# Places for 2304 instead of 2560 edges in a sender block: the fifth tile of each block spread over 128 partitions as two pairs of slots

## The reference, cut to what matters

```python
h = relu(x @ proj.T + b)                                # block 0, two message passes
for l in range(2):
    trans = einsum('nh,tdh->tnd', h, edge_W[l])
    agg = segment_sum(trans[edge_type, src], dst)
    h = relu(gru_cell(agg, h, ...))
x = layernorm(x + h @ out_w.T + out_b)
# block 1, three passes: messages W_r x[src], mean for each (type, target), root, residual
for W, root, b in ...:
    agg = segment_sum(xw[etype, src] * norm[:, None], dst)
    h = res + relu(relu(agg + h @ root + b))
x = layernorm(x + h)
x = layernorm(x + gcn(x))                               # block 2, sums at the senders, scaled by degrees
x = layernorm(x + mlp([x, mean attributes at sender, mean attributes at target]))   # block 3
```

## Time and profile before

| | |
|---|---|
| median of 3 runs | 2967.55 us (2962.49 to 2968.0) |
| the profiled execution, span from first to last instruction | 2969.2 us |
| PE busy | 2492.2 us (84%) |
| DVE busy | 1808.3 us (61%) |
| POOL busy | 1585.9 us (53%) |
| ACT busy | 868.5 us (29%) |
| chain that ended last | PE 69%, issue 10%, DMA 7%, DVE 6% |
| transfers | 520.11 MB, mean 175 GB/s |

### The profile page before, as it was taken

How to read it: one execution, slowest core, us unless ns; L and a number is a source line. 1 busy time by engine, 2 the same in 40 slices (tenths; PEclk the granted TensorE clock), 3 DMA queues, 4 the chain that set the end, 5 groups by cost and what they waited for, 6 DMA issues and landing times.

```text
span 2969.2 us, 45704 instructions
## 1 busy us (share of the span) xinstructions
PE 2492.2 (84%) x15625; PEld 2211.7 (74%) x15625; DVE 1808.3 (61%) x6126; ACT 868.5 (29%) x1546; POOL 1585.9 (53%) x1706
## 2 busy tenths in 40 slices
PE   7587878888687899746999998998989897878798
PEld 3366666666387889436999997888988886777797
DVE  4565656575576777423876655676865554433585
ACT  2355555554354111213222231111311110443102
POOL 0656666663577666542566626666456665565200
PEclk9789888888799999857999999999999999898899
DMA  7312112110398666106888887877788774565793
GB/s 273 111 50 53 51 51 53 51 52 25 103 281 260 166 173 170 38 27 210 274 272 270 269 266 231 240 228 211 238 273 251 226 234 134 174 213 198 232 267 105
DMA packets 271515, 520.11 MB, mean 175 GB/s; under 512 B 61999, under 2 KB 115554, under 8 KB 270501
## 3 DMA queue, kind: packets, MB, share of 16 engines
q1 hardware_dynamic: 185053, 289.49, 31.2%
q0 software_dynamic: 86224, 227.59, 26.6%
HBM read 323.93 MB, written 192.99 MB: 174 GB/s over the span
## 4 chain that ended last, share of the span: by engine, by line
PE 69%; issue 10%; DMA 7%; DVE 6%; another core or an unknown queue 4%; ACT 2%; POOL 2%; SPq 0%; DVEq 0%; POOLq 0%; ACTq 0%
PE ps L1058 21%; PE ps L1030 10%; PE ps L892 7%; PE ps L1043 6%; PE ps L1245 5%; PE ps L1289 4%; PE ps L886 4%; PE ps L878 4%; DMA chunks<-xs 2%; DMA rec<-chunks,idx 2%; DMA srow<-lanes_of_slots 1%; DVE shot L2033 1%; POOL attributes L744 1%; PE ps L1112 1%
## 5 line engine op out<-in xcount | busy, mean ns | idle before, releaser
L735 POOL DMA_INDIRECT rec<-chunks,idx x596 | 588.5, 987 | 500.5 <-PE ps L1058 184.9
L1058 PE MATMUL ps<-dhot,rec 128*128 128x168 f32 x4768 | 757.2, 312 | 70.4 <-issue 35.3
L1058 PEld LDWEIGHTS ps<-dhot,rec 128*128 128x128 f32 x4768 | 703.8, 194 | 99.6 <-issue 77.6
L2054 DVE TENSOR_SCALAR dhot<-iota,dcode 128x168 f32<-128x168 f32 x2384 | 584.6, 311 | 216.7 <-remote 102.4
L1030 PE MATMUL ps<-hrow,shot 126*128 126x128 f32 x4000 | 516.3, 284 | 63.8 <-issue 29.5
L735 POOL DMA_INDIRECT msg<-messages,idx_buf x416 | 398.2, 957 | 307.3 <-issue 189.7
L1030 PEld LDWEIGHTS ps<-hrow,shot 126*128 126x128 f32 x4000 | 493.7, 199 | 81.7 <-issue 65.9
L1386 ACT ACTIVATE xs<-ps 128x512 f32<-128x512 f32 x500 | 295.1, 597 | 763.5 <-PE ps L1030 393.8
L744 POOL DMA_INDIRECT attributes<-w,rank_to x352 | 353.2, 1004 | 213.1 <-issue 102.2
L2033 DVE TENSOR_SCALAR shot<-srow,lane_no 126x512 f32<-126x512 uint8 x500 | 230.2, 486 | 117.4 <-PE ps L1030 51.2
L892 PE MATMUL ps<-big,lane1h 128*128 128x300 f32 x832 | 231.6, 432 | 9.3 <-issue 8.0
(11 more groups left out here) (304 smaller groups left out, 2538.6 us busy)
## 6 DMA issues: line engine op xcount, KB each, us to landing
chunks<-xs SPq DMA_DIRECT2D x375, 256.0 KB
tmp<-inverse_counts SPq DMA_DIRECT2D x36, 1008.0 KB
chunks<-xs SPq DMA_DIRECT2D x125, 258.0 KB
srow<-lanes_of_slots SPq DMA_DIRECT2D x100, 320.0 KB
grec<-chunks SPq DMA_DIRECT2D x125, 256.0 KB
messages<-big SPq DMA_DIRECT2D x25, 504.0 KB
trow<-lanes_of_targets SPq DMA_DIRECT2D x30, 320.0 KB
rec<-chunks,idx POOLq DMA_INDIRECT x596
```

The source lines that it names most:

```text
L735: eng.indirect_dma_start(buf, None, table, bass.IndirectOffsetOnAxis(ap=index, axis=0)).then_inc(sem, 16)
L1058: last = mm(ps[:, 4 + i % 2, (v % 3) * WT:(v % 3 + 1) * WT], rec[:, v % RS, j * P:(j + 1) * P], dhot[:, v % DS, j * WT:(j + 1) * WT], star ...
L2054: last = vec.tensor_scalar(dhot[:, v % DS, j * WT:(j + 1) * WT], iota[:, 0:WT], dcode[:, v, j:j + 1], None, ALU.is_equal)
```

## The change

A block now has 2304 places: four tiles of 128 records and a fifth of 64 records. The fifth tile's 64 records of 4 slots are laid over 128 partitions with 2 slots each: partitions 0 to 63 hold slots 0 and 1, partitions 64 to 127 slots 2 and 3. So the fifth tile has 2 columns, in `srow`, `shot`, the products, ACT's copy, the codes and the one-hot rows of the senders' sums. In DRAM a record stays a row of 4 slots, so each half is stored and loaded by a transfer of its own with 64 rows. The last 12 rounds of the first loop work out the partition and column of ranks from 2048 on by six more steps.

```diff
-NTILE = NQ * 4
+FULL = NQ - TB
+NTILE = 4 * FULL + 2 * TB
+LANE_ROWS = -(-NTILE // 4)
-CAP = QS * SPAN
+HALF = P // 2
+BLOCK_RECS = (QS - 1) * P + HALF
+CAP = 4 * BLOCK_RECS
-RECS = NQ * P
+RECS = TB * BLOCK_RECS
...
+        def slot_cols(n):
+            return 4 if n < FULL else 2
+        def puts(k, n):
+            return 1 if n < FULL else 4 if k == 1 else 2
...
                 def store_tile(k, i):
+                    if n < FULL:
+                        eng.dma_start(x1_d[at:at + P, 0:cols], xs[:, i % XS, 0:cols])
+                    else:
+                        for z in range(2):
+                            lanes, to = slice(z * HALF, (z + 1) * HALF), slice(2 * z * P, 2 * (z + 1) * P)
+                            eng.dma_start(x1_d[at:at + HALF, to], xs[lanes, i % XS, 0:2 * P])
+                            if k == 1:
+                                codes = slice(4 * P + 2 * z, 4 * P + 2 * z + 2)
+                                eng.dma_start(x1_d[at:at + HALF, codes], xs[lanes, i % XS, 4 * P:4 * P + 2])
...
-            eng.dma_start(srow_d.rearrange("(i c) p -> c i p", c=NQ), srow_u8[0:NQ])
+            eng.dma_start(srow_d.rearrange("(i c) p -> c i p", c=LANE_ROWS), srow_u8[0:LANE_ROWS])
...
             for i in range(NQ):
+                if by_record(i) < FULL:
+                    eng.dma_start(to[:, 0:4 * P], x1_d[at:at + P, 0:4 * P])
+                    eng.dma_start(to[:, 4 * P:], attr_d[4 * at:4 * (at + P), :].rearrange(...))
+                else:
+                    rows_ = x1_d[at:at + HALF, 0:4 * P].rearrange("l (m z c) -> z l m c", z=2, c=2 * A)
+                    for z in range(2):
+                        eng.dma_start(to[lanes, 0:2 * P].rearrange("p (m c) -> p m c", c=2 * A), rows_[z])
+                        eng.dma_start(to[lanes, 2 * P:2 * (P + A)], attrs[z])
...
-                for j in range(4):
+                for j in range(slot_cols(tile_no(k, i))):
                     last = mm(ps[...], shot[...], hrow[0:BS, sb_, :], start=True, stop=True)
...
-                    act(xs[:, i % XS, 0:4 * P], ps[:, STAGE1_BANKS[i % 3], :], ACT.Copy)
+                    cols = slot_cols(tile_no(k, i)) * P
+                    act(xs[:, i % XS, 0:cols], ps[:, STAGE1_BANKS[i % 3], 0:cols], ACT.Copy)
...
+                    last_round = g >= NEAR_STEPS[-1]
+                    if last_round:
+                        st.did(vec.tensor_scalar(rank_i[:, 4, :], rank_i[:, 0, :], 1, 1, ...))
+                        st.did(vec.tensor_scalar(rank_half[:, 0, :], ranks_g, float(4 * P * (QS - 1)), None, ALU.is_ge))
...
+                        st.did(vec.tensor_tensor(rank_half[:, 1, :], rank_half[:, 0, :], rank_i[:, 4, :], ALU.mult))
+                        st.did(vec.tensor_tensor(rank_half[:, 0, :], rank_half[:, 0, :], src_sb[...], ALU.mult))
+                        st.settle()
+                        st.did(vec.scalar_tensor_tensor(out=slot_lane[...], in0=rank_half[:, 1, :], ...))
+                        st.do(vec.tensor_tensor(rank_half[:, 0, :], rank_half[:, 0, :], rank_half[:, 1, :], ALU.add))
+                        st.do(vec.scalar_tensor_tensor(out=rank_hi[:], in0=rank_half[:, 0, :], scalar=-2.0, ...))
```

More of the change, by code:

```diff
@@ L251, in graph_kernel @@
             no_rows = one("no_rows", [P, RANKS // P])
-            rank_i = one("rank_i", [P, 4, G], I32)
+            rank_i = one("rank_i", [P, 5, G], I32)
+            rank_half = one("rank_half", [P, 2, G])
             slot_lane = one("slot_lane", [P, SUB, G])
@@ L417, in every_fifth, with first_col, by_record, first_record @@
             return buf[:, first:first + YW * (NYB - 2) + 1:YW]
-        def tile_slots(i):
-            return (i % QS) * QCOLS + i // QS * 4
+        def slot_cols(n):
+            return 4 if n < FULL else 2
+        def first_col(n):
+            return 4 * n if n < FULL else 4 * FULL + 2 * (n - FULL)
+        def by_record(i):
+            return i % QS * TB + i // QS
+        def first_record(n):
+            return n % TB * BLOCK_RECS + n // TB * P
+        def puts(k, n):
+            return 1 if n < FULL else 4 if k == 1 else 2
+        def all_puts(s, runs):
+            return sum(puts(k, n) for k in range(1, runs + 1) for n in range(s, NQ, XS))
+        def put_wait(eng, k, i):
+            s = i % XS
+            eng.wait_ge(q(f"x1_stored_{s}"), 16 * (all_puts(s, k - 1) + sum(puts(k, n) for n in range(s, i + 1, XS))))
         def targets_got(eng, c):
@@ L430, in record_got @@
             s = i % GR
-            eng.wait_ge(q(f"x1_stored_{s}"), 16 * (4 * len(range(s, NQ, XS)) + 2 * (i // GR + 1)))
+            loads = sum(1 if by_record(n) < FULL else 2 for n in range(s, i + 1, GR))
+            eng.wait_ge(q(f"x1_stored_{s}"), 16 * (all_puts(s, 4) + 2 * loads))
         def record_put(eng, v):
@@ L866, in first_loop @@
                 eng.sem_inc(q("count_mm"), SUB)
-                mm(ps[:, 7, 0:NTILE], wt("ones"), lanes_flat[:, GE:GE + NTILE], start=True, stop=False, skip_group_check=True)\
+                mm(ps[:, 7, 0:QS * QCOLS], wt("ones"), lanes_flat[:, GE:GE + QS * QCOLS], start=True, stop=False,
+                   skip_group_check=True)\
                     .then_inc(q("placed"), 1)
@@ L1154, in _ @@
                     for j in range(4):
-                        last = mm(ps[0:NQ, 7, j * P:(j + 1) * P], src1[:, j * NQ:(j + 1) * NQ], wt("ident"), start=True,
-                                  stop=True)
+                        last = mm(ps[0:LANE_ROWS, 7, j * P:(j + 1) * P], src1[:, j * LANE_ROWS:(j + 1) * LANE_ROWS], wt("ident"),
+                                  start=True, stop=True)
                     last.then_inc(q("lanes_mm"), 1)
@@ L1286, in _ @@
                 record_got(eng, i)
-                for j in range(4):
-                    got = grec[:, i % GR, :].rearrange("p (m s a) -> p s m a", s=4, a=A)[:, j]
+                cols = slot_cols(by_record(i))
+                for j in range(cols):
+                    got = grec[:, i % GR, 0:cols * (P + A)].rearrange("p (m s a) -> p s m a", s=cols, a=A)[:, j]
                     last = mm(ps[0:BS, 6 + b % 2, 0:P + A], ghot[:, i % GH, j, :], got, start=first_tile and j == 0,
-                              stop=last_tile and j == 3)
+                              stop=last_tile and j == cols - 1)
                 last.then_inc(q("gcn_sum"), 1)
@@ L1382, in keep_tile @@
                     if i >= XS:
-                        slot_wait(eng, "x1_stored", XS, k, NQ, i - XS)
+                        put_wait(eng, k, i - XS)
                     elif k >= 3:
-                        slot_wait(eng, "x1_stored", XS, k - 1, NQ, range(i, NQ, XS)[-1])
-                    act(xs[:, i % XS, 0:4 * P], ps[:, STAGE1_BANKS[i % 3], :], ACT.Copy).then_inc(q("x1_evac"), 1)
+                        put_wait(eng, k - 1, range(i, NQ, XS)[-1])
+                    cols = slot_cols(tile_no(k, i)) * P
+                    act(xs[:, i % XS, 0:cols], ps[:, STAGE1_BANKS[i % 3], 0:cols], ACT.Copy).then_inc(q("x1_evac"), 1)
                 def keep_sums(k, gi):
@@ L2036, in slot_hot @@
                         after(eng, "shot", k, i + 1)
[L2037 removed]
+                        st.did(vec.tensor_reduce(deg_part[0:BS, n:n + 1], shot[0:BS, i % SS, 0:cols], AX.X, ALU.add))
                     if k == 1 and i in beside:
@@ L2211, in slot_hots @@
                     eng.wait_ge(q("gcn_sum"), i - GH + 1)
-                for j in range(4):
-                    at = tile_slots(i) + j
+                for j in range(slot_cols(by_record(i))):
+                    at = first_col(by_record(i)) + j
                     last = vec.tensor_scalar(ghot[:, i % GH, j, :], iota[:, 0:BS], gcn_lo[:, at:at + 1], None, ALU.is_equal)
```

75 lines of the change are left out of this document (49 added, 26 removed).

## The result

The changed kernel takes 3038.56 us (median of 4 runs, 3029.7 to 3068.16), the kernel before 2967.78 beside it: a ratio of 1.0243, 95% interval 1.0188 to 1.0298. That is 71 us slower, where I forecast 7, and above the range.

The account below looks back on a forecast made before the run. PE was taken as the limit in layer 2, with POOL also near its limit in layers 3 and 4, and SP next, close behind PE. Terms +16 +15 -27 +3 = +7 us on 2967.55 gave 2974; range 2940 to 2996.

Parts of the forecast that it names:

- two terms of the sum: Fifth tiles of layer 1 and sums at the senders, both longer through SP's issues: +16 and +15 us.
- The half transfer, 0.42 us: On SP, a 64-row transfer was taken to cost 0.42 us, between 0.30 for 25 rows and 0.48 for 128.
- Sums at the senders, +15: SP would need 6.19 us a block instead of 5.52, making this stage 15 us longer; bounds 7 less, 29 more.
- My special price for 512 pieces: At the sums at the senders, SP's next transfer was taken to start 0.62 us behind each load of 512 pieces.
- Products of layers 2 to 4, -27: Halved fifth-tile products on PE would save 11.2 us in layer 2 and 8 each in layers 3 and 4.
- First loop, +3: Six more small DVE steps in each of the last 12 rounds would add 3 us, bounds 0 and 9.
- At nothing: The store of the lanes (113 partitions instead of 125) and the shorter clearing of attributes would change nothing.
- SP is cheap for halves: Rival: 64 rows cost SP 0.30 us in layer 1 and the sums; -27 us, 2940; chance 0.22.
- SP sets nothing: Rival: POOL and ACT pace layer 1, transfer engines the sums at 5.04 us a block; -36 us, 2931; chance 0.04.
- POOL holds layers 3 and 4: Rival: only layer 2 gives its 11 us of saved products; +23 us, 2990; chance 0.15.
- Small pieces cost more: Rival: on SP, 0.83 us behind each 512-piece load and 0.48 for a half; +27 us, 2994; chance 0.12.
- 200 s - 53: Layer 1 plus sums at the senders, in us, with s the start to start of a half transfer on SP.

Follow-up runs that it names:

- e1: Changed kernel with 24 of layer 1's full tiles stored in several pieces of various lanes and columns; 3058.74 us in its one execution.
- e5: Changed kernel with ACT instead of SP issuing layer 1's second-half rows and codes of fifth tiles and all attribute loads at the sums; ratio 1.0047.
- e4: Kernel before with two of the four products of each fifth tile left out in layers 2 to 4, nothing else changed; ratio 1.0006.
- e7: Kernel before without the attribute sends of layers 2 to 4, all products kept; ratio 0.9402.
- e6: Kernel before with fifth tiles' products halved and the attribute sends left out in layers 2 to 4; ratio 0.9321.

## Why the prediction was wrong

**The direction was right, by two terms of the sum; its size was not.** 74 us were lost where I said 31, and 27 of gain that I set against them never came.

**The half transfer, 0.42 us: wrong, and out of its bounds.** I took 0.30 for 25 rows and 0.48 for 128 as ends and went between. It is 0.64, above both. In layer 1 100 x (0.64 - 0.42) = 22 us are the whole distance from the 984.0 forecast for the first gather to 1006.38. The mechanism (SP's four issues a tile, ACT and POOL waiting for stores, the gather behind them) was as described; the term was mis-sized. The step that failed is the assumption that the cost rises with rows, so that neighbours in row count bound it; e1 shows 32 and 128 lanes at 0.42 and 64 at 0.59.

**Sums at the senders, +15: +33.** The four half loads take 2908.61 - 2905.96 = 2.65 us, not 2.08, and the transfer behind them 0.63 from start to start instead of 0.48. That is 0.72 more a block, 18 us over 25, the miss. My special price for 512 pieces (0.62, measured 0.65) happened to be near; it is no property of the pieces, since rows and attributes cost the same, and stores of 1 KB rows too. The floor by the transfer engines, 5.04 us a block, was not refuted: e5 ends at 132.7, 5.3 a block, with them 0.90 busy.

**Products of layers 2 to 4, -27: about 0.** e4 measured the term alone: 1.0006. I had read that PE is the limit in layer 2 from its 74.00 busy of 74.00 us, and that POOL is not from 48.70 busy of 74. Both rows are true, and the conclusion was not. PE was at its pace there: 567 records in 80 us before, 573 in 80 in e7, 495 in 70 in e6, 7.1 to 7.2 a us, but 496 in 79 in e4, 6.3. So a second chain, one that goes with the sends, was as long as PE's work, and I gave the whole of PE's saving. POOL's 48.70 busy of 74 do not show that chain. What PE alone would give was reckoned well for layer 2, 11.2 us against the 10 of e6; that 27 for three layers is near the 26.2 of e6 is luck, as the 8 us of layers 3 and 4 were set by POOL's floor. In layers 3 and 4 I saw POOL near its floor, and took 8 of at most 9 us all the same. The bound from below should have been 0, as the rival's reason applied to all layers.

**First loop, +3: nothing.** Its last L946 starts at 741.2, L892 at 741.7 before. DVE's 96.46 us instead of 88.59 put nothing off.

**At nothing:** right for lanes and attributes: the first tile's product starts at 805.0, 806.7 before.

**The rivals.** SP is cheap for halves: out, with 0.60 an issue and 0.64 from start to start. SP sets nothing: out, by e5, which gives 39.6 us of the sums back by moving issues alone. POOL holds layers 3 and 4: the gain did not come there, and not in layer 2 either; e7 shows that POOL's sends have a part in it. Small pieces cost more: right in sign. The true case is both of these and a dearer half transfer, and I had priced each rival with the other terms left at their middle. With 0.64 in my own formula, 200 s - 53, the two SP terms give 75 us, against 74 measured. Its mechanism holds; that it fits so closely is partly luck, since it gives 38 to layer 1 (40.6) and 37 to the sums (33.3), where it has 0.2 us behind 512 pieces that is not there. And with the products at about 0 the whole is 200 s - 50, which changes sign at s = 0.25 and not at 0.38: by it even the cheap half transfer of 0.30 would have made the kernel slower.

## What to carry to other kernels

Before a transfer is split into partition halves, count its issues on its queue: each costs the queue a fixed time, here more than that of the whole. Spread them over a second engine that is idle in that stage before the saving on the bound engine is booked. And where an engine is busy all the time, ask whether leaving out some of its work alone, the others as they are, moves the end: one such run (e4) was worth more than all busy shares. Count in the trace what a run leaves out before its gain is divided by it; I had 224 sends where it was 304.
